# A state-space stage on one core: the next sequence's step sizes moved in among the last group's skips, their turned sums in another PSUM bank, and the decay sums ahead of the output projection

## What is computed

```python
zxbcdt = X @ W_in.T
z, xBC, dt = jnp.split(zxbcdt, [D_INNER, D_INNER + CONV_DIM], axis=-1)
dt = jax.nn.softplus(dt + dt_bias)
xBC = silu(causal_depthwise_conv(xBC, conv_w) + conv_b)      # 4 taps
x, Bm, Cm = jnp.split(xBC, [D_INNER, D_INNER + D_STATE], axis=-1)
dA = jnp.exp(dt * -jnp.exp(A_log))
# h = h * dA_t + dt_t * B_t x_t ;  y_t = C_t h      over the tokens
y = ys + D * xh
y = y * jax.nn.silu(z)
y = y * rsqrt(mean(y * y) + EPS) * norm_w
out = y @ W_out.T + X
```

## Time and profile before

| what | value |
|---|---|
| median of three executions | 1976.39 us (1974.3 to 1978.3) |
| profiled execution: time | 1981.6 us |
| profiled execution: span from first to last instruction | 1979.9 us |
| PE busy | 1870.4 us (94%) |
| DVE busy | 1418.0 us (72%) |
| ACT busy | 1230.5 us (62%) |
| POOL busy | 466.4 us (24%) |
| mean granted PE clock | 0.976 |

### The profile page before, as it was taken

The page is one execution under the profiler, slowest core; times in us unless marked ns, Lnnn a source line. Parts: engine busy times, 40 slices in busy tenths (PEclk is TensorE's granted clock), DMA queues, the critical chain, the costliest instruction groups (busy, mean ns, idle before and its releaser), DMA issues. The chain is left out here.

```text
span 1979.9 us, 38486 instructions
## 1 busy us (share of the span) xinstructions
PE 1870.4 (94%) x12588; PEld 1280.7 (65%) x12588; DVE 1418.0 (72%) x2857; ACT 1230.5 (62%) x3068; POOL 466.4 (24%) x661
## 2 busy tenths in 40 slices
PE   7799999999999999868999999999999999899988
PEld 5657676767676766545566666666666664578853
DVE  7878787878787878536767677767676766556448
ACT  4445454454545453417888889888989887366514
POOL 2212121212222222331132222222222223100006
PEclk9999999999999999889999999999999998899999
DMA  7222222213131303242334343434242422731166
GB/s 219 62 56 92 53 95 52 96 42 106 35 112 29 118 20 104 88 124 70 104 91 123 89 126 89 126 79 137 77 139 77 129 76 83 221 139 43 65 208 259
DMA packets 120044, 200.60 MB, mean 101 GB/s; under 512 B 23088, under 2 KB 44592, under 8 KB 119600
## 3 DMA queue, kind: packets, MB, share of 16 engines
q1 hardware_dynamic: 110640, 179.20, 29.5%
q0 software_dynamic: 9216, 18.89, 3.8%
HBM read 117.27 MB, written 29.88 MB: 74 GB/s over the span
## 5 line engine op out<-in xcount | busy, mean ns | idle before, releaser
L1900 DVE TENSOR_REDUCE a_mx<-a_shared 128x1 f32<-128x512 f32 x512 | 329.5, 681 | 56.6 <-PE a_shared L2029 54.4
L1837 ACT ACTIVATE a_shared<-a_shared,a_mx 128x512 f32<-128x512 f32 x512 | 340.8, 668 | 22.2 <-DVE a_mx L1900 21.8
L1830 ACT ACTIVATE a_probs<-a_scores 128x512 f32<-128x512 f32 x512 | 300.1, 599 | 75.4 <-PE a_scores L2047 72.1
L1127 PE MATMUL m_outp<-m_wout,m_g 128*128 128x512 f32 x512 | 225.9, 600 | 2.7 <-issue 2.7
L2029 PE MATMUL a_shared<-a_ks,a_qs 96*128 96x512 f32 x512 | 208.7, 428 | 13.9 <-ACT a_shared L1837 10.0
L2047 PE MATMUL a_scores<-a_qs,a_ks 98*128 98x512 f32 x512 | 204.5, 412 | 5.8 <-ACT a_probs L1830 5.6
L2002 PE MATMUL a_shared<-link 128*128 128x512 f32 x768 | 200.8, 398 | 7.4 <-POOL a_ident L1753 6.3
L676 DVE SCALAR_TENSOR_TENSOR m_acc<-m_proj,m_cw,m_acc 128x511 f32<-128x511 f32 (+2 forms) x216 | 158.8, 747 | 53.2 <-ACT m_acc L492 48.1
L553 ACT ACTIVATE m_xw<-m_added,m_wdt 128x64 f32<-128x64 f32 x256 | 55.9, 330 | 217.5 <-DVE m_xdt L764 217.5
L967 PE MATMUL m_proj<-m_xt_hi,link 128*128 128x512 f32 x448 | 182.2, 407 | 1.0 <-DVE m_acc L676 0.9
L2029 PEld LDWEIGHTS a_shared<-a_ks,a_qs 96*128 96x128 f32 x512 | 94.5, 190 | 129.2 <-ACT a_shared L1837 57.6
(11 more groups left out here) (279 smaller groups left out, 3618.0 us busy)
## 6 DMA issues: line engine op xcount, KB each, us to landing
m_dec<-step_decay SPq DMA_DIRECT2D x64, 256.0 KB, 4.0
a_qs<-link SPq DMA_DIRECT2D x256, 64.0 KB, 2.0
m_ce<-run_decay SPq DMA_DIRECT2D x128, 112.0 KB, 3.5
a_ks<-a_k_hi POOLq DMA_DIRECT2D x192, 64.0 KB, 2.5
e_x<-x SPq DMA_DIRECT2D x11, 1024.0 KB, 5.7
m_xt_in<-x_t_in SPq DMA_DIRECT2D x8, 1024.0 KB, 7.3
m_x_tok<-x_in SPq DMA_DIRECT2D x8, 1024.0 KB, 5.5
x<-m_x_tok SPq DMA_DIRECT2D x32, 256.0 KB, 2.2
```

Source lines behind the costliest of these rows:

```text
L1127: ins = pe.matmul(outp[t % 2][:, :], g[:, k, t * P:(t + 1) * P], wout[:, k, :], start=(k == 0), stop=(k == XT_TILES - 1))
L1830: act.activation(probs[:, n % 2, h, :], scores[t.score_bank(n, h)][:, :], ACT.Exp, scale=-1.0).then_inc(exp_ready, 1)
L1837: act.activation(scored[:, :], scored[:, :], ACT.Exp, scale=-1.0, bias=mx[:, i % 2, j, h:h + 1], accum_out=den[:, i, j, h:h + 1]).then_inc ...
L1900: dve.tensor_reduce(mx[:, i % 2, j, h:h + 1], bank(what)[:, :], AX.X, ALU.min).then_inc(mx_ready, 1)
```

## The change

It touches four programs of the state-space stage and no arithmetic.

- PE: `turn_steps` writes to `steps = proj[0]` instead of `turn`, so that it no longer waits for the states; it stands ahead of the B/C tile instead of behind the carried outputs. x tile 0, which overwrites `proj[0]`, waits for `raw_sizes` to have read it (`dtv`). `decay_sums` stands ahead of `out_proj(b, 0)`, and `mean_square` between the two z tiles of group 0. 
- DVE: `raw_sizes` stands ahead of the B/C convolution, `softplus` behind it, both ahead of the last group's skips; `step_sizes` stands between the skips and the gates. `running_decays` goes ahead of the first x convolution, `head_weights` between the two. In `between`, scaled x goes ahead of the norm of the last output tile.
- ACT: the copy of the raw steps goes ahead of the squares of group 2, the exponent and logarithm and the first tap of x tile 0 and the decays ahead of the last squares, and the silus of B and C behind them.
- The head of sequence 0 keeps its order, but for the bank and the new wait.

```diff
+        steps = proj[0]
```

ACT:

```diff
+            def next_head(done, b):
+                step_exponents(b)
+                x_tap0(b, False, 0)
+                decays(b, False)
+                squares(done, False, NG - 1)
+                bc_silus(b, False)
+                x_tap0(b, False, 1)
+                xc_silus(b, False, 0)
                 z_silus(b, 0)
...
                     weighted_x(b, first, gr)
+                    if gr + 1 == NG and more:
+                        raw_steps(b + 1, False)
...
                     elif more:
-                        raw_steps(b + 1, False)
                         bc_tap0(b + 1, False)
...
-                squares(b, first, NG - 1)
                 if more:
-                    head(b + 1, False)
+                    next_head(b, b + 1)
                 else:
+                    squares(b, first, NG - 1)
```

DVE:

```diff
-                                                turn[:, 0:CH * NH].rearrange("p (c h) -> p c h", h=NH),
+                                                steps[:, 0:CH * NH].rearrange("p (c h) -> p c h", h=NH),
...
                     if gr + 1 == NG and more:
+                        raw_sizes(b + 1, False)
                         conv(b + 1, 8, 1, 1, 1)
+                        softplus(b + 1)
                     skip_added(b, first, gr, 0)
...
                     skip_added(b, first, gr, 1)
...
+                    if gr + 1 == NG and more:
+                        step_sizes(b + 1, False)
                     gated(b, gr)
...
                 if more:
-                    raw_sizes(b + 1, False)
-                    softplus(b + 1)
-                    step_sizes(b + 1, False)
+                    running_decays(b + 1, False)
                     conv(b + 1, 0, 2, 0, 2)
+                    head_weights(b + 1)
                     conv(b + 1, 1, 3, 1, 3)
                 norm_scale(b)
-                if more:
-                    running_decays(b + 1, False)
                 norm(b, 0)
                 if more:
-                    head_weights(b + 1)
                     head_products(b + 1)

             def between(done, b):
-                for gr in range(3):
+                for gr in range(2):
                     local_decays(b, gr)
                     norm(done, gr + 1)
+                local_decays(b, 2)
                 scaled_x(b, False, 0)
+                norm(done, TT - 1)
                 apply_norm(done)
                 next_convs(b, 0)
```

PE:

```diff
                 elif n == 2:
-                    pe.wait_ge(dt_read, at(b, 1, 1))
+                    pe.wait_ge(dtv, at(b, DT_STEPS, 1))
...
             def turn_steps(b, first):
-                if not first:
-                    pe.wait_ge(st_ready, turn_free)
...
-            def decay_sums(b):
+            def decay_sums(b, first):
+                if not first:
+                    pe.wait_ge(st_ready, at(b, NG * (NC - 1), 0))
                 pe.wait_ge(a_ready, at(b, 1, 1))
...
                     elif more:
+                        turn_steps(b + 1, False)
                         in_proj(b + 1, False, 1, COL_BC)
                     carried_outputs(b, gr)
                 if more:
-                    turn_steps(b + 1, False)
                     for n in range(2):
                         x_tile(b + 1, False, n)
+                    decay_sums(b + 1, False)
                 out_proj(b, 0)
+                if more:
+                    z_tile(b + 1, False, 0, 0)
                 mean_square(b)
                 if more:
-                    decay_sums(b + 1)
-                    for j in range(2):
-                        z_tile(b + 1, False, 0, j)
+                    z_tile(b + 1, False, 0, 1)
                     products(b + 1, False)
                 for t in range(1, TT):
                     out_proj(b, t)
```

More of the change, by code:

```diff
@@ L581, in decays, with step_exponents @@
                 ins.then_inc(wd_ready, 1)
-            def head(b, first=True):
-                if first:
-                    x_high(b, True)
-                    act.wait_ge(small_in, 16 * N_SMALL)
-                    act.activation(aneg[:, :], aneg[:, :], ACT.Exp).then_inc(dta, 1)
-                    raw_steps(b, True)
-                    bc_tap0(b, True)
+            def step_exponents(b):
                 act.wait_ge(dtv, at(b, DT_STEPS, 3))
@@ L594, in head, with bc_silus @@
                 act.activation(sm[:, 4], sm[:, 3], ACT.Ln).then_inc(dta, 1)
[L595 to L596 removed]
+            def bc_silus(b, first):
                 act.wait_ge(conv_read, at(b, 9, 1))
@@ L604, in head @@
                 act.activation(ct[NS:P, :], acc[NS:P, 1, :], ACT.Silu).then_inc(bc_ready, 1)
-                if not first:
-                    x_tap0(b, False, 0)
-                x_tap0(b, first, 1)
-                if not first:
-                    xc_silus(b, False, 0)
-                decays(b, first)
-                if first:
-                    xc_silus(b, True, 0)
+            def head(b):
+                x_high(b, True)
+                act.wait_ge(small_in, 16 * N_SMALL)
+                act.activation(aneg[:, :], aneg[:, :], ACT.Exp).then_inc(dta, 1)
+                raw_steps(b, True)
+                bc_tap0(b, True)
+                step_exponents(b)
+                x_tap0(b, True, 0)
+                bc_silus(b, True)
+                x_tap0(b, True, 1)
+                decays(b, True)
+                xc_silus(b, True, 0)
+                z_silus(b, 0)
+            def next_head(done, b):
+                step_exponents(b)
+                x_tap0(b, False, 0)
[4 more added lines that the diff above has]
+                xc_silus(b, False, 0)
                 z_silus(b, 0)
@@ L1073, in turn_steps @@
             def turn_steps(b, first):
-                turn_free = value(pe, at(b, NG * (NC - 1), 0))
-                raw_dt = value(pe, at(b, 1, 1))
-                met(pe, w_used, 1)
-                pe.wait_ge(dt_read, raw_dt)
-                if not first:
-                    pe.wait_ge(st_ready, turn_free)
+                pe.wait_ge(dt_read, at(b, 1, 1))
                 for c in range(CH):
-                    ins = pe.matmul(turn[:, c * NH:(c + 1) * NH], dt_ch[:, c * P:(c + 1) * P], pair_sum[:, :],
+                    ins = pe.matmul(steps[:, c * NH:(c + 1) * NH], dt_ch[:, c * P:(c + 1) * P], pair_sum[:, :],
                                     start=True, stop=True)
```

4 lines of the change are left out of this document (1 added, 3 removed).

## The result

| | kernel before | changed kernel |
|---|---|---|
| median | 1976.39 us (1974.3 to 1981.35, 5 runs) | 1987.28 us (1982.31 to 1988.32, 5 runs) |
| the same again, in a later comparison | 1977.48 us (23 runs) | 1985.28 us (1982.92 to 1988.97, 6 runs) |
| profiled execution, time and span | 1981.6 and 1979.9 us | 1982.31 and 1980.6 us |
| mean granted clock of TensorE | 0.976 | 0.978 |

The ratio is 1.0041, 95% interval [1.0023, 1.006], and 1.0044 [1.0028, 1.006] in the second comparison: 8 to 9 us slower. I had forecast +2.9 us. Medians tell more here than the two profiled executions, which differ by 0.7 us only: they lie at the upper end of the kernel before and at the lower end of the changed one.

The account below looks back on a forecast made before the run. TensorE was taken to bound the state-space stage. Losses of 7.7 + 0.7 = 8.4 us less a gain of 5.5 made +2.9 us: 1984.5 us from the profiled 1981.6, 1979.3 from the median 1976.4; range 1971.5 to 1987 us.

Parts of the forecast that it names:

- forecast near cancellation: State-space stage: losses of 8.4 us against a gain of 5.5 us leave +2.9 us; chance 0.55.
- late silus: Rival: B/C silus come late, TensorE waits again at the second z tile, 0.3 to 1.0 us per sequence; chance 0.17.
- What closes: First head group: earlier scaled x ends the states before TensorE wants them; gain 0.79 us per sequence, 5.5 us in all.
- Step 1: Sequence end: turned steps delay the B/C tile 0.99 us; its convolution frees VectorE at 415.22; x tile 0 loses nothing.
- step 4: Sequence end, TensorE: decay sums and output projection wait for step sizes and gates; 1.1 us lost per sequence, 7.7 in all.
- Step 2: Sequence end, VectorE: softplus ahead of the last skips, away from GpSimd's sums, takes 1.43 us instead of 1.87.
- Step 3: Sequence end, VectorE: skips 1.32 us, step sizes 1.40, gates 1.28, so the gates end at 420.65.
- Step 5: TensorE: the mean square alone between two z tiles costs some 0.1 us per sequence, 0.7 us in all.
- The cover of the second z tile: Its convolution ends at 430.91, TensorE arrives at 431.2: 0.3 us of cover, so no wait.
- The clock: Rival: TensorE's clock drops at the new gap, 1.4 us lost per sequence, 10 us in all, 1989; chance 0.03.
- The sum: Whole kernel: loss 7.7 + 0.7 = 8.4 us, gain 5.5 us, together +2.9 us.

Follow-up runs that it names:

- after_pad64: Changed kernel with 64 more waiting instructions in ScalarE's program at an idle place ahead of the attention stage; 1979.04 us, ratio 1.0006 to the kernel before.
- between_only: Kernel before with only scaled x put ahead of the norm of the last output tile in `between`; 1973.84 us, ratio 0.9977.
- bank_only: Kernel before with only the steps turned in `proj[0]` ahead of the B/C tile and raw sizes ahead of its convolution; 1988.67 us, ratio 1.0051.
- mean_first: Changed kernel with the mean square ahead of both z tiles instead of between them; 1985.64 us, ratio 1.0034 to the kernel before.
- all_but_between: Changed kernel with the old order in `between`, the last norm ahead of scaled x again; 1991.59 us, ratio 1.0069 to the kernel before.
- before_pad126: Kernel before with 126 more waiting instructions in ScalarE's program at an idle place ahead of the attention stage; 1983.38 us, ratio 1.0025.
- after_again: Changed kernel run again without any edit; 1985.28 us, ratio 1.0044 to the kernel before.

## Why the prediction was right and wrong

By the ratio the time is 1976.39 x 1.0041 = 1984.5 us, in the upper part of the range (1971.5 to 1987); the changed kernel's median alone, 1987.28, lies 0.3 us above it. The outcome, slower by more than 0.2%, had a chance of 0.40, that of no difference 0.48. The forecast near cancellation was right for the stage that I had looked at: the period rose by 0.22 us, where +2.9 us over seven sequences meant 0.41. With the stop out of the way the whole is +1.2 us, -1.4 to +3.8 (`after_pad64`). That the time came out in the upper part of the range is luck: that part was meant for the late silus, and what filled it is a stop in another stage. By the steps:

- **What closes.** Right, and by the chain that was forecast: scaled x comes 0.64 us behind the turn instead of 2.18, the states end 14.01 us behind it where 14.07 was forecast (368.3 - 354.23). 0.79 us forecast, 0.85 in the trace, 0.83 in the period of `between_only`.
- **Step 1.** The B/C convolution frees VectorE at 415.67 - 0.43 = 415.24; forecast 415.22. That the delay of the tile costs nothing by itself holds for x tile 0 only. On ScalarE's chain, which hangs on it too, it costs 0.8 us per sequence when made alone (`bank_only`); the change takes that chain apart and pays in step 4 and at the second z tile. I had not priced that chain.
- **Step 2.** Right in kind: L708 and L715 take 0.20 and 0.18 us where their like took 1.32 and 0.66 beside GpSimd's sums. `bank_only`, where only the first of the two moved away from the sums, confirms it: 0.20 us for the moved one, 0.63 for the other, which started at 424.00 beside sums that ran from 421.88 for 2.70 us. Softplus took 416.85 - 415.67 = 1.18 us; forecast 1.43.
- **Step 3.** From start to start, skips 1.22 (forecast 1.32), step sizes 1.28 (1.40), gates 1.29 (1.28). Steps 2 and 3 were each a tenth or two too long, since I had taken them with the gaps of their old place. In the new one the next instruction starts before the last small one has ended: the skips at 416.85 where the reciprocal runs to 416.93, the gates at 419.35 where `a` runs to 419.48.
- **Step 4.** Mechanism right, size smaller for that reason: 0.73 us lost ahead of the output projection, 1.1 forecast.
- **Step 5.** Open: 0.1 us forecast, and no run shows it. In both orders of `mean_first` and the changed kernel the second z tile waits for its convolution, which hides a tenth.
- **The cover of the second z tile.** The convolution was forecast for 430.91 and ended at 431.05 (431.48 - 0.43). TensorE came 0.4 us earlier than forecast, because step 4 was smaller, and so met it: 0.26 us of waiting. The two waits were coupled. What the first does not take, the second does: 0.73 + 0.26 = 0.99, forecast 1.1 + 0. The rival of the late silus came true in part, at the low end of its 0.3 to 1.0 us.
- **The clock.** It did not drop at these waits. But the price given for it, 1.4 us for one drop, fits what `bank_only` and `all_but_between` show: sequences of 103.2 and 103.1 us beside their others of 101.63 and 101.84.
- **The chances.** Half of the silus' case, 0.17, is 0.085 and not 0.12; with it slower had 0.37 and no difference 0.51.
- **The sum.** The step that failed is one that isn't in it: I counted table loads as time on ScalarE only, and took all stages behind the changed one as fixed. The two loads fewer move the code behind them, and this is worth 4 to 5 us, about half of the result or a little more.

That the position of ScalarE's loop decides is shown in both directions. Over thirteen profiles, the starts 764 and 826 have stops of 2.50 to 3.86 us and attention in 774.3 to 776.1 us; the starts 762 and 890 have 4.80 to 6.38 us and 780.0 to 782.7 us.

The traces also show where in the stop the difference lies. The sequencer's rows give the branch back at the loop's end and the first two instructions of its body (register operations), ahead of the exponential. First the changed kernel, where the exponential starts at 1320.29:

```profile
L1498 ACTq COMPARE_BRANCH  x1: 45/45/45, 1314.0 to 1314.0; - x1
L1498 ACTq FUSED_REGOPS  x1: 73/73/73, 1317.3 to 1317.3; - x1
L1839 ACTq FUSED_REGOPS  x1: 37/37/37, 1317.4 to 1317.4; - x1
```

then `before_pad126`, where it starts at 1322.28:

```profile
L1490 ACTq COMPARE_BRANCH  x1: 50/50/50, 1316.0 to 1316.0; - x1
L1490 ACTq FUSED_REGOPS  x1: 73/73/73, 1319.4 to 1319.4; - x1
L1831 ACTq FUSED_REGOPS  x1: 37/37/37, 1322.2 to 1322.2; - x1
```

All thirteen profiles have a first stop behind the branch, 3.0 to 4.4 us to the first instruction of the body. The eight short ones have no other: the exponential follows 0.2 us later. The five long ones have a second stop of 2.4 to 2.9 us, behind the second instruction when the loop starts at 762, behind the first in `before_pad126`. So there is a border in the program just behind the start of the loop, and another like it about 128 instructions on. (The trace of `before_pad126` has 127 instructions more ahead of the loop than the kernel before, a branch besides the 126; with it the two borders are 128 apart.) That the code is fetched anew there, in pieces of 8 KB, is inferred: the packets of the instruction queue carry 8 KB each, and three of them fall into each of the five long stops, one or two into each of the eight short ones; but this queue serves all engines, and the profile doesn't say whose code a packet is.

What stays open: the profiled executions give 1.5 us in the changed stage and 4.8 in attention (1.1 and 3.9 in the pair taken again), 5 to 6 us of the 8 to 9 of the medians. Behind attention the changed kernel is 5.6 us shorter in the first pair and 2.5 longer in the second, and single runs of one kernel differ by 8 us and more, so the rest can't be placed.

## What to carry to other kernels

Read a change's effect on every stage, not only on the one it edits. An added or dropped instruction, a table load that the compiler inserts included, shifts all code behind it on that engine, and the turn of a long loop can cost twice as much from one position as from another; if a result is off by some microseconds, compare stages of unchanged code first, and undo the shift with a few waits at an idle place. Of two waits in a row on the pacing engine the second is covered by the first: price them together, as the later of two chains, not one by one. When a change has several parts, run each alone: here one small part was the whole gain, and another, made alone, cost in the changed stage almost four times what the whole change did.

## What the runs showed of the hardware

- ScalarE stops for 2.5 to 3.9 or for 4.8 to 6.4 us at the one turn of a long loop, by the loop's place in its program: a first stop of 3.0 to 4.4 us behind the branch, and in the long case a second of 2.4 to 2.9 us one or two instructions into the body (13 profiles).
- Waits of TensorE of 1.2 and 1.6 us near 1315 (kernel before, `after_pad64`) left the clock at 1.00; waits of 2.8 and 3.8 us (`after_again`, changed kernel) were followed by 0.66 over 1320 to 1330 us. In the state-space stage waits of 0.6 to 0.7 us were followed by a lower clock now and then (three times in the profile of `bank_only`, once in `all_but_between`, twice in `before_pad126`) and mostly by none. Each time this cost 1.3 to 1.6 us. The clock of the third stage differs from execution to execution by more: 0.70 and 1.00 from 1660 to 1700 us in two profiles of the kernel before, whose third stages take 348.3 and 341.5 us.
- A small VectorE instruction (128x64 tensor_scalar) took 1.32 and 0.66 us beside GpSimd's sums, 0.20 and 0.18 us away from them.
- The table loads took 1.28 us in every place, with the next instruction 0.01 us behind the earlier trace rows, 425.02 + 1.28 to 426.31 above, unless that one waited for another engine. The Trainium skill ("ScalarE: Activation LUTs", What ACT_TABLE_LOAD costs) adds a drain of about 1.38 us to a switch; the trace of the changed kernel does not show it either.
